# A graph layer on one core: 25 of 49 edge counts moved to ScalarE, and scatter positions made in five pieces

## The reference

```python
edge_index = jnp.stack([src, dst])            # 206250 edges, 6250 nodes
xn = _layernorm(x, axis=-1)
# graph attention, 4 heads: idx_i = src, idx_j = dst
Wh = (h @ W.T + b).reshape(N, HEADS, HEAD_DIM)
e = leaky_relu(alpha_src[idx_i] + alpha_dst[idx_j], 0.2)
ex = jnp.exp(e - segment_max(e, idx_i)[idx_i])
att = ex / segment_sum(ex, idx_i)[idx_i]
out = segment_sum(att[:, :, None] * Wh[idx_j], idx_i)
x = x + out + mix(xn)
x = x + ffn(_layernorm(x, axis=-1))
```

## Time and profile before

| | us |
|---|---|
| median of three runs | 3393.16 |
| lowest and highest | 3389.64, 3396.11 |
| time of the profiled execution | 3393.59 |
| its span, first to last instruction | 3391.8 |
| DVE busy | 1906.6 (56%) |
| POOL busy | 2156.6 (64%) |
| PE busy | 2288.1 (67%) |
| ACT busy | 773.7 (23%) |

### The profile page before, as it was taken

How to read it: one execution, slowest core, us unless ns; L and a number is a source line. 1 busy time by engine, 2 the same in 40 slices (tenths; PEclk the granted TensorE clock), 3 DMA queues, 4 the chain that set the end, 5 groups by cost and what they waited for, 6 DMA issues and landing times.

```text
span 3391.8 us, 41019 instructions
## 1 busy us (share of the span) xinstructions
PE 2288.1 (67%) x10919; PEld 1564.2 (46%) x10920; DVE 1906.6 (56%) x3902; ACT 773.7 (23%) x1397; POOL 2156.6 (64%) x2140
## 2 busy tenths in 40 slices
PE   0000466664477787877878787877877878787877
PEld 0000233332355555555555555555555555555555
DVE  5999321212455656556665656556664565646564
ACT  0000122221132222222222222222222222222222
POOL 0002777401676777777777777777777777777771
PEclk9555677877698988888899998989897988998888
DMA  2200011102333343444434443443434444343453
GB/s 64 108 0 1 26 44 32 38 28 52 103 94 106 100 122 101 109 115 102 122 102 123 103 122 102 109 117 102 123 101 106 120 102 122 102 122 102 111 108 38
DMA packets 271469, 305.58 MB, mean 90 GB/s; under 512 B 164198, under 2 KB 210796, under 8 KB 271020
## 3 DMA queue, kind: packets, MB, share of 16 engines
q0 software_dynamic: 97760, 251.60, 27.9%
q1 hardware_dynamic: 140038, 18.08, 3.4%
q10 hardware_dynamic: 33480, 33.36, 3.0%
HBM read 276.25 MB, written 26.62 MB: 89 GB/s over the span
## 4 chain that ended last, share of the span: by engine, by line
PE 39%; POOL 15%; DVE 11%; issue 9%; ACT 2%; DMA 1%; DVEq 0%; POOLq 0%; SPq 0%; ACTq 0%
PE sum_banks L937 20%; POOL gathered L863 15%; PE f_banks L952 8%; DVE onehot L1340 3%; PE turned L909 2%; PE f_banks L996 1%; DVE gathered L1361 1%; PE f_banks L1071 1%; DMA gathered<-table,col 1%; PE sum_banks L925 1%; PE f_banks L977 1%; PE f_banks L1072 1%; PE f_banks L978 1%; PE f_banks L966 1%; DVE he L1489 1%
## 5 line engine op out<-in xcount | busy, mean ns | idle before, releaser
L863 POOL DMA_INDIRECT gathered<-table,col x1872 | 1898.5, 1014 | 595.1 <-issue 564.5
L937 PE MATMUL sum_banks<-gathered,onehot 128*128 128x260 f32 x3744 | 1061.8, 446 | 104.9 <-DVE gathered L1361 104.0
L937 PEld LDWEIGHTS sum_banks<-gathered,onehot 128*128 128x128 f32 x3744 | 818.4, 224 | 294.9 <-issue 132.5
L1361 DVE TENSOR_TENSOR gathered<-gathered 128x512 f32<-128x512 f32 x936 | 591.4, 692 | 47.2 <-ACT gathered L1116 44.4
L1340 DVE TENSOR_TENSOR onehot<-iota_row,col 128x1024 f32<-128x1024 f32 x236 | 289.0, 1225 | 472.7 <-PE sum_banks L937 442.9
L270 POOL DMA_INDIRECT edge_list<-payload,pos x244 | 248.0, 1016 | 377.9 <-DVE pos L387 300.6
L1112 ACT COPY onehot_t<-turned 128x1024 bf16<-128x1024 bf16 x236 | 238.7, 1011 | 392.0 <-PE turned L909 391.4
L1126 ACT COPY acc<-sum_banks x234 | 88.0, 376 | 877.3 <-PE sum_banks L937 726.5
L909 PE MATMUL turned<-ident_bf,onehot 128*128 128x128 bf16 x1888 | 158.5, 232 | 190.2 <-DVE onehot L1340 189.8
L582 PE MATMUL bank<-ident,y 128*128 128x128 f32 x104 | 25.6, 427 | 278.0 <-DVE y L469 278.0
L909 PEld LDWEIGHTS turned<-ident_bf,onehot 128*128 128x128 bf16 x1888 | 116.1, 103 | 208.4 <-DVE onehot L1340 169.7
(11 more groups left out here) (304 smaller groups left out, 2722.6 us busy)
## 6 DMA issues: line engine op xcount, KB each, us to landing
gathered<-table,col POOLq DMA_INDIRECT x1872
table<-wh ACTq DMA_DIRECT2D x13, 520.0 KB, 3.1
xn<-y ACTq DMA_DIRECT2D x13, 512.0 KB, 2.9
xn_batch<-xn ACTq DMA_DIRECT2D x13, 512.0 KB, 4.0
x_all<-in_x SPq DMA_DIRECT2D x1, 6144.0 KB
x_batch<-in_x ACTq DMA_DIRECT2D x12, 512.0 KB
out<-xf ACTq DMA_DIRECT2D x12, 512.0 KB
edge_list<-xn_all SPq DMA_DIRECT2D x2, 2176.0 KB, 13.8
```

The source lines that it names most:

```text
L863: g.indirect_dma_start(gathered[:, l, t, :], None, sh["table"], bass.IndirectOffsetOnAxis(ap=col[l][:, t // G, t % G, 0:1], axis=0)).then_ ...
L937: last = t.matmul(sum_banks[:, ds(banks_of[g], 1), 0:TB].rearrange("p a w -> p (a w)"), onehot[:, l % 3, g * G + k, :], gathered[:, l, g * ...
L1361: v.tensor_tensor(value, value, gathered[:, l, tiles, C:TB].unsqueeze(3).broadcast_to([P, G, H, HD]), ALU.mult).then_inc(s_mul, 1)
```

## The change

The counting of blocks is divided. DVE counts blocks 0 to 24 as before. ACT makes, for each b from 24 to 48, the sum over the edges of the sign of (b + 0.5 − block of the edge), which is the number of edges in blocks up to b less the number above it; `balance` holds these 25 sums. DVE then takes differences of neighbouring sums and halves them, which gives counts 25 to 48. POOL makes the 49 bias columns `edge_of`. DVE clears a part of `balance`, and this instruction carries the new signal `s_bucket` that releases ACT.

The making of the payload moves behind the table `shift` and is done in pieces, together with the lookup of positions. The pieces are 16, 57, 57, 57 and 57 windows instead of four of 61 for the lookups and one of 244 for the payload. POOL waits for `s_pos` at the first window of each piece.

```diff
-PART, PARTS = WINDOWS // 4, 4
+FIRST_PART, PART = 16, 57
+PART_ENDS = (FIRST_PART, *range(FIRST_PART + PART, WINDOWS + 1, PART))
+ON_ACT = 24
...
+            step(g.tensor_scalar(edge_of[:, :], iota_row[:, 0:NB], 0.5, None, ALU.add))
...
-                if w % PART == 0:
-                    pool.wait_ge(s_pos, w // PART + 1)
+                if w == 0 or w in PART_ENDS:
+                    pool.wait_ge(s_pos, 1 + sum(end <= w for end in PART_ENDS))
...
+            v.memset(balance[:, 0:ON_ACT], 0.0).then_inc(s_bucket, 1)
...
-            for b in range(NB):
+            for b in range(ON_ACT + 1):
                 if b >= 2:
                     dve.wait_ge(s_counts, b - 1)
                 v.tensor_scalar(hit[b % 2], bucket, iota_row[:, b:b + 1], 0.0, ALU.is_equal, ALU.add,
                                 accum_out=counts[:, b:b + 1]).then_inc(s_counts, 1)
-            dve.wait_ge(s_counts, NB)
+            dve.wait_ge(s_counts, ON_ACT + 1)
+            dve.wait_ge(s_balance, NB - ON_ACT)
+            rising = slice(ON_ACT + 1, NB)
+            step(v.tensor_tensor(counts[:, rising], balance[:, rising], balance[:, ON_ACT:NB - 1], ALU.subtract))
+            step(v.tensor_scalar(counts[:, rising], counts[:, rising], 0.5, None, ALU.mult))
...
-            for part in range(PARTS):
-                mine = slice(part * PART, (part + 1) * PART)
+            for part, end in enumerate(PART_ENDS):
+                first = PART_ENDS[part - 1] if part else 0
+                some, mine, edges = end - first, slice(first, end), slice(first * Q, end * Q)
+                entries, other = keys[0][:, edges].bitcast(I32), keys[1][:, edges]
+                v.tensor_scalar(win_i[:, mine], entries.rearrange("p (w e) -> p w e", e=Q)[:, :, 0], 20, DEAD,
+                                ALU.logical_shift_right, ALU.bitwise_and)
+                v.tensor_scalar(payload[:, edges, 0], entries, (1 << 13) - 1, None, ALU.bitwise_and)
...
                 v.tensor_copy(pos[:, mine], place).then_inc(s_pos, 1)
                 dve.wait_ge(s_pos, part + 1)
...
+            act.wait_ge(s_const, 1)
+            act.wait_ge(s_bucket, 1)
+            for b in range(ON_ACT, NB):
+                i = b - ON_ACT
+                if i >= 2:
+                    act.wait_ge(s_balance, i - 1)
+                s.activation(above[i % 2], bucket, ACT.Sign, bias=edge_of[:, b:b + 1], scale=-1.0,
+                             accum_out=balance[:, b:b + 1]).then_inc(s_balance, 1)
```

More of the change, by code:

```diff
@@ L71 @@
 assert NBP - NB >= 2
-assert TE + PAD_SLOTS <= SLOTS and WINDOWS == PART * PARTS and GR % Q == 0
+assert TE + PAD_SLOTS <= SLOTS and WINDOWS == PART_ENDS[-1] and GR % Q == 0
 assert NO_TARGET == 52 * P and NB * P <= 1 << 13 and NO_TARGET < 1 << 13
@@ L118, in stage_sort_and_mix @@
         int_tmp = keys[1][:, 0:TE].bitcast(I32)
+        above = [keys[0][:, i * (TE // 2):(i + 1) * (TE // 2)].bitcast(BF16) for i in range(2)]
         hit = [keys[1][:, i * (TE // 2):(i + 1) * (TE // 2)].bitcast(BF16) for i in range(2)]
@@ L126, in stage_sort_and_mix @@
         key_of = sb("key_of", [P, NB], I32)
+        edge_of = sb("edge_of", [P, NB])
+        balance = sb("balance", [P, NB])
         lives = sb("lives", [P, NB, Q - 1], BF16)
@@ L185, in stage_sort_and_mix @@
         s_scat = (s_scat0, s_scat1)
+        s_bucket, s_balance = sem("s_bucket"), sem("s_balance")
         block = ctx.enter_context(nc.Block())
@@ L346, in _ @@
             assert now == 0
[L348 to L358, removed]
             dve.wait_ge(s_base, 1)
@@ L378, in _ @@
             step(v.tensor_scalar(shift[:, NB:NBK], node_col[:, :], float(WINDOWS), float(LIST // Q), ALU.mult, ALU.add))
-            for part in range(PARTS):
-                mine = slice(part * PART, (part + 1) * PART)
[L381 to L387, removed]
+            for part, end in enumerate(PART_ENDS):
[5 more added lines that the diff above has]
+                v.tensor_scalar(payload[:, edges, 0], entries, (1 << 13) - 1, None, ALU.bitwise_and)
+                step(v.tensor_scalar(other.bitcast(I32), entries, 13, P - 1, ALU.logical_shift_right, ALU.bitwise_and))
+                v.tensor_copy(win_b[:, mine], win_i[:, mine])
+                step(v.tensor_copy(payload[:, edges, 1].bitcast(F32), other.bitcast(I32)))
+                step(v.tensor_scalar(win_b[:, mine], win_b[:, mine], float(NB), None, ALU.min))
+                step(v.tensor_scalar(other, payload[:, edges, 0], float(NO_TARGET), NO_NODE, ALU.is_ge, ALU.mult))
+                step(v.tensor_tensor(payload[:, edges, 1].bitcast(F32), payload[:, edges, 1].bitcast(F32), other, ALU.add))
+                of, place = lookup[:, 0:some, :], pos_f[:, 0:some]
+                step(v.tensor_tensor(of, win_b[:, mine].unsqueeze(2).broadcast_to([P, some, NBK]),
+                                     iota_row[:, 0:NBK].unsqueeze(1).broadcast_to([P, some, NBK]), ALU.is_equal))
+                step(v.tensor_tensor(of, of, shift[:, :].unsqueeze(1).broadcast_to([P, some, NBK]), ALU.mult))
+                step(v.tensor_reduce(place, of, AX.X, ALU.add))
+                step(v.scalar_tensor_tensor(place, place, float(first), iota_row[:, 0:some], ALU.add, ALU.add))
+                v.tensor_copy(pos[:, mine], place).then_inc(s_pos, 1)
```

## The result

The changed kernel takes 3354.71 us (median of four runs, 3349.0 to 3361.92), against 3394.64 us for the kernel before in the same comparison: a ratio of 0.9885, with a 95% interval of 0.9866 to 0.9904. The forecast was 3357. The profiled execution took 3353.68 us (span 3351.9), 39.9 us less than the one of before.

What follows compares the result with a forecast made beforehand. DVE's unbroken chain into the turns was taken to bound stage one, with POOL's scatters slack; −42.95 + 4.6 + 1.0 + 1.0 = −36.4 us from 3393.6 gave 3357 us, range 3350 to 3366, or 3345 to 3371 with the clock's cases.

Steps and rivals of the forecast that it cites:

- The bound: Stage one: DVE's entry into the turns sets its end, not POOL, whose last scatter starts some 174 us before.
- Part one: Block counts: DVE loses 24 of 49 and gains small steps, net −42.95 us; ACT costs 0, range 0 to 1.7.
- Parts two and three: Payload and lookups in five pieces: repeated fixed costs on DVE, +4.6 us for the payload, +1.0 for the lookups.
- Part four: DVE beside scatters during payload of pieces two to five: waiting costs +1 us, range 0 to 3.9.
- the rival that scatters lock DVE out: Pieces two to five: 28 DVE instructions each wait for a 0.96 us scatter, +27 us, 3383 in all; chance 6%.
- The rest: Signs in the profile: first scatter near 259, POOL's last near 590, turns start near 325, stage one ends near 778.
- the sum: Whole kernel: the four parts' terms, −42.95 + 4.6 + 1.0 + 1.0 = −36.4 us.
- The rival of a slower kernel: Counts: accumulating Sign on ACT too slow, DVE waits; break-even 3.27 us each, at 4 us 3412 in all; chance 3%.
- The rival of PE's clock: Turns and stage two: shifted turns add or spare low-clock spells, giving 3342 to 3350 or 3365 to 3375; chance 14%.
- a spell: In the turns: one turn at low PE clock, 39.1 us instead of 33.9, costing 5.1 us.

Runs made afterwards that it cites:

- The single runs: The counts alone (turns start 5.64 us before the changed kernel's) and the pieces alone (5.74 us after those of the kernel before).
- the pieces alone: Kernel before with payload and lookups in five pieces, all 49 counts on DVE: 3393.14 us, ratio 1.0013.
- the counts alone: Changed kernel with payload in one go and lookups as before the change, only the counts divided: 3350.84 us, ratio 0.9876.
- the balanced counts: The counts alone, divided at block 23, with a one-column Sign on ACT ahead of its wait: 3344.79 us, ratio 0.9865.

## Why the prediction was right

**The bound.** That DVE's chain into the turns sets the end of stage one, and POOL doesn't, is shown from both sides: 174 us of delay for the scatters cost nothing, and 67 us taken out of DVE's chain took 56 off the time.

**Part one.** −42.95 was forecast; `runs` is made at 84.04 instead of 127.20, −43.16. ACT takes 1.622 us for a sum where I took 1.7 between bounds of 1.60 and 1.83: the accumulator read costs its engine next to nothing here. The table load did fall behind the release, which I had only in the range; ACT was still ready, at 80.3, 3.3 us before DVE. The rule of the Trainium skill weighed there ("ScalarE: Activation LUTs", section "Rules for kernel authors") puts simple operations on VectorE; it names relu, max, min, add and mul. It doesn't carry over to this form, a comparison whose results are summed: 1.81 us on DVE, 1.62 on ACT.

**Parts two and three.** Forecast +4.6 and +1.0. The pieces take 55.89 us, payload and lookups took 7.76 + 42.50: +5.63. The single runs agree (5.64 and 5.74).

**Part four.** This term was too large: I took 1 us of 0 to 3.9. Beside the pieces it measured 59.23 − 59.14 = 0.1 us, and the tables behind the lookups took 15.25 instead of 15.06, 0.2 more. The reading under it was off as well. The worst step in the kernel before was not the one of 5 elements at 0.33 us, which takes 0.23 without scatters, but the copy of 13 elements into `it_end`, 0.40 against 0.17; the forecast compared with a step of another shape, for want of a kernel without scatters. What stretched most were POOL's scatters, to 2.9 us beside DVE's lookups and to 1.3 at most away from them. So the rival that scatters lock DVE out is refuted at its price, 0.96 us for each of 28 instructions, though some of DVE's small steps do stretch, by up to 0.2 us in the tables. The 1.38 us of the normalisation, which the forecast set against the rival, didn't show that. The rule of the Trainium skill weighed there ("SBUF — State Buffer", section "Who interferes with whom") has a VectorE instruction in a two-port mode and a GpSimd one exclude each other for a whole instruction; no step of DVE read here stretched by the length of a scatter.

**The rest.** Turns start at 323.75 (forecast near 325), first scatter 258.7 (259), last 584.3 (590), stage one ends at 778 (778). What the sum leaves, −37.3 against −39.9 measured in the profiled executions, lies in the turns (−0.9) and behind them (−1.7), within what the runs of one kernel differ by.

**The rival of a slower kernel.** That ACT would be too slow was refuted at the change's size, and its mechanism confirmed where it was made true: 41 sums cost 23.0 us.

**The rival of PE's clock.** Here the forecast was partly lucky. The profiled executions before and after each have two turns of 39 us, so the turns took 452.57 and 451.68; nothing in the working said that they would match. The rival priced a spell at 5.1 us and allowed one or two. The profiled execution of the pieces alone lost more, 34 us in the turns, as the last section shows; the median of its thirteen executions, 3393.14, wasn't moved by that.

## What to carry to other kernels

Find what sets the end of a stage before crediting an edit with helping an engine: here the part of the change that fed POOL earlier cost 5.6 us of the 43 gained, since POOL had 174 us to spare already. When an engine does a long serial preparation and then mostly waits inside a loop, look whether the preparation's consumers have slack; if so, lay it into the loop's waits, which was worth more than the change itself. Count on ScalarE as a second adder for long reductions, at 1.62 us for 1612 elements, and put a one-column call of the same function ahead of the wait, so that the table load falls into idle time; that pays where ScalarE is the later of the two.

## What the runs showed of the hardware

I had expected turns of 33.9 us with a single one of 39.1 now and then. They can also lock into 37.5 us. In the profiled execution of the pieces alone the square roots of successive turns on ACT stand so:

```profile
592.15 0.20 ACT L523 ACTIVATE std<-inv 128x4 f32<-128x4 f32 x1 [0.96 <-DVE inv L468]
629.70 0.20 ACT L523 ACTIVATE std<-inv 128x4 f32<-128x4 f32 x1 [0.91 <-DVE inv L468]
667.22 0.20 ACT L523 ACTIVATE std<-inv 128x4 f32<-128x4 f32 x1 [0.96 <-DVE inv L468]
```

Ten of its twelve turns are 37.5 to 37.7 us long, and all 13 take

```profile
366.82:853.44 486.62, 332.08 (x832) 166.22 (x832) 94.56 (x339) 107.42 (x246) 196.41 (x205) 0.73 0.10 31
```

with the same instructions on PE as the 452.57 us of the kernel before, at a mean granted clock of 0.73 instead of 0.78. PE is busy 332.08 us instead of 299.14 and idle 154.5 instead of 153.4, so nearly all of the 34 us are products that take longer, not waits. Within a turn PE is granted half its clock (1.2 of 2.4 GHz) at first, after its wait for DVE's normalised rows, and the full clock later. One long turn of this kernel, and one turn of 33.9 us of the kernel before, in stretches (PE busy, PEclk, DMA share, GB/s):

```profile
667.22:688.50 21.28, 16.23 (x32) 0.52 0.07 25
688.50:703.50 15.00, 9.46 (x33) 1.00 0.07 24
```

```profile
606.64:618.50 11.86, 8.56 (x18) 0.50 0.16 50
618.50:639.00 20.50, 13.48 (x47) 0.99 0.06 17
```

The half clock lasts 21 us of the one turn and 12 of the other. The longest executions are those with the lowest clock: 3436.49 us at a mean of 0.824, 3420.51 at 0.829, the others of that kernel at 0.836 to 0.840. Short rows of such turns, 37.1 to 37.8 us, stand in the counts alone (three) and in the profiled execution of the balanced counts (seven, at 3371.62 us, where the other five took 3343.79 to 3346.76) as well. What decides whether the turns lock wasn't settled; it is larger than most of the terms of this study, and it is why the small steps were read from the trace and not from medians.
